# VectorE instead of GpSimd multiplies silu(gate) by the up projection in the last stage of a decoder layer

## The reference

```python
def _reorder_quantize_x(x, idx):
    scale = jnp.max(jnp.abs(x)) / GLOBAL_DIV
    xr = (x / scale)[:, idx]
    scale_x = jnp.max(jnp.abs(xr), axis=1, keepdims=True) / FP8_MAX
    qx = _fp8(xr / scale_x)
    return (qx, scale_x, scale)
...
qx, sx, sc = _reorder_quantize_x(xf, up_reorder_index)
g = _qlinear(qx, sx, sc, w_gate, up_reorder_index, out_idx=down_reorder_index)
u = _qlinear(qx, sx, sc, w_up, up_reorder_index, out_idx=down_reorder_index)
t = jax.nn.silu(g) * u
qt, st, sct = _reorder_quantize_x(t, down_reorder_index)
y = _qlinear(qt, st, sct, w_down, down_reorder_index)
...
x = x + _L0_attn_ref(_layernorm(x, axis=-1), ...)
x = x + _L0_xattn_ref(_layernorm(x, axis=-1), ctx_2048, mask_BxS2_bk0)
x = x + _L0_ffn_ref(_layernorm(x, axis=-1), ...)
```

## Time and profile before

| What | Value |
|---|---|
| Time before, median of 3 runs | 3047.39 us (3046.95 to 3049.8) |
| Profiled execution: time | 3048.07 us |
| Profiled execution: span | 3046.3 us |
| PE busy | 2735.2 us (90%) |
| DVE busy | 2197.3 us (72%) |
| ACT busy | 1124.8 us (37%) |
| POOL busy | 861.0 us (28%) |
| Mean granted TensorE clock | 0.944 |

### The profile page before, as it was taken

How to read it: one execution, slowest core, us unless ns; L and a number is a source line. 1 busy time by engine, 2 the same in 40 slices (tenths; PEclk the granted TensorE clock), 3 DMA queues, 4 the chain that set the end, 5 groups by cost and what they waited for, 6 DMA issues and landing times. The chain is left out here.

```text
span 3046.3 us, 40207 instructions
## 1 busy us (share of the span) xinstructions
PE 2735.2 (90%) x14796; PEld 2244.7 (74%) x14796; DVE 2197.3 (72%) x3911; ACT 1124.8 (37%) x1838; POOL 861.0 (28%) x815
## 2 busy tenths in 40 slices
PE   3289999999999999999999999996259999999985
PEld 1178888888888888888888888885146666666652
DVE  6567777677677777777777777775946888788785
ACT  2123333333333333333333333332544555555553
POOL 1211121121121121121112112113813666665665
PEclk7599999999999999999999999997579999999997
DMA  4533242333233233324233323322443343333410
GB/s 150 188 152 125 83 160 83 125 122 121 102 141 111 98 126 117 125 90 152 84 128 118 122 101 115 110 98 67 121 146 111 115 118 115 125 114 118 117 54 18
DMA packets 110754, 348.99 MB, mean 115 GB/s; under 512 B 12000, under 2 KB 12128, under 8 KB 101600
## 3 DMA queue, kind: packets, MB, share of 16 engines
q1 hardware_dynamic: 108224, 337.76, 32.0%
q0 software_dynamic: 2336, 8.65, 1.0%
HBM read 249.92 MB, written 96.47 MB: 114 GB/s over the span
## 5 line engine op out<-in xcount | busy, mean ns | idle before, releaser
L720 PE MATMUL bank<-attention_xT,attention_w_hi 128*128 128x512 f32 x3072 | 951.3, 391 | 9.5 <-POOL attention_w_lo L587 5.7
L620 POOL TENSOR_TENSOR attention_sq_sum<-attention_sq_sum,attention_sq 128x512 f32<-128x512 f32 x128 | 208.7, 1631 | 1609.8 <-ACT attention_sq L691 1609.8
L720 PEld LDWEIGHTS bank<-attention_xT,attention_w_hi 128*128 128x128 f32 x3072 | 569.3, 188 | 122.9 <-issue 11.1
L720 PE MATMUL bank<-attention_xT,attention_w_lo 128*128 128x512 f32 x1536 | 599.9, 391 | 0.0
L729 PE MATMUL bank<-attention_w_hi,attention_xT 128*128 128x256 f32 x2048 | 372.9, 283 | 2.6 <-DVE attention_vl L813 2.6
L1201 PE MATMUL bank<-w_out_hi,finish_og 128*128 128x512 f32 x1024 | 353.9, 408 | 8.3 <-DMA finish_og<-gated_heads 6.5
L720 PEld LDWEIGHTS bank<-attention_xT,attention_w_lo 128*128 128x128 f32 x1536 | 289.0, 188 | 62.5
L729 PEld LDWEIGHTS bank<-attention_w_hi,attention_xT 128*128 128x128 f32 x2048 | 317.7, 191 | 2.9 <-DVE attention_vl L813 2.8
L839 DVE TENSOR_TENSOR attention_sf<-bank,attention_dcy 128x512 f32<-128x512 f32 (+1 forms) x256 | 147.9, 619 | 218.4 <-PE bank L746 218.4
L729 PE MATMUL bank<-attention_w_lo,attention_xT 128*128 128x256 f32 x1024 | 289.4, 283 | 0.0
L858 DVE SCALAR_TENSOR_TENSOR attention_og<-bank,attention_nw,attention_gate 128x512 f32<-128x512 f32 x128 | 96.2, 751 | 255.7 <-PE bank L767 255.7
(11 more groups left out here) (194 smaller groups left out, 5134.2 us busy)
## 6 DMA issues: line engine op xcount, KB each, us to landing
attention_xT<-normed_turned SPq DMA_DIRECT2D x62, 2048.0 KB, 8.8
gated_heads<-attention_og_out SPq DMA_DIRECT2D x64, 1024.0 KB, 7.5
finish_og<-gated_heads SPq DMA_DIRECT2D x128, 512.0 KB, 3.8
normed_turned<-attention_xT SPq DMA_DIRECT2D x8, 2048.0 KB, 7.3
attention_og_out<-in_x SPq DMA_DIRECT2D x8, 1024.0 KB, 9.6
attention_raw<-in_w_head SPq DMA_DIRECT2D x16, 512.0 KB, 9.4
finish_x<-in_x SPq DMA_DIRECT2D x32, 256.0 KB, 4.3
out<-finish_x SPq DMA_DIRECT2D x32, 256.0 KB, 4.3
```

The costliest lines, as they stand in the source:

```text
L620: g.tensor_tensor(sq_sum[:, col], sq_sum[:, col], sq[:, :], ALU.add).then_inc(s_acc, 1)
L720: mm = pe.matmul(dst[:, :], part[a][w][:, k, col:col + P], xT[i][:, b, k, :], start=(k == 0 and s == 0), stop=(k == KD - 1 and s == 2))
```

## The change

The three products `silu_up(n, 0)`, `silu_up(n, 1)` and `silu_up(n, 2)` leave POOL's order. The same three instructions, with the same operands and the same waits, are issued by DVE: the first behind `x_scale(n + 2)` and ahead of the third `scaled_gate_up`, the second between `t_round_sum(n - 1)` and `t_round_out(n - 1)`, the third behind `denominator(n + 3)` and ahead of `t_scale(n)`. POOL keeps `silu`, `rstd` and `add_ffn`. Nothing else is edited.

```diff
                     if tile(n):
-                        silu_up(n, 0)
                         silu(n, 1)
-                        silu_up(n, 1)
                         silu(n, 2)
-                        silu_up(n, 2)
...
+                def silu_up(m, i):
+                    k, (a, w) = m * NF + i, FS[i]
+                    v.wait_ge(s_gs, k + 1)
+                    v.wait_ge(s_u, k + 1)
+                    if m:
+                        v.wait_ge(s_ts, m)
+                    v.tensor_tensor(t_[:, a:a + w], g_[k % 2][:, 0:w], u_[k % 2][:, 0:w], ALU.mult).then_inc(s_t, 1)
...
                         x_scale(n + 2)
                     if tile(n):
+                        silu_up(n, 0)
                         scaled_gate_up(n, 2)
                     if tile(n - 1):
                         t_round_sum(n - 1)
+                    if tile(n):
+                        silu_up(n, 1)
+                    if tile(n - 1):
                         t_round_out(n - 1)
...
                         denominator(n + 3)
                     if tile(n):
+                        silu_up(n, 2)
                         t_scale(n)
```

More of the change, by code:

```diff
@@ L1041, in silu @@
                     g.tensor_tensor(g_[k % 2][:, 0:w], g_[k % 2][:, 0:w], sg[k % 2][:, 0:w], ALU.mult).then_inc(s_gs, 1)
[L1043 to L1049, removed]
                 def rstd(n):
```

## The result

The changed kernel is slower: 3056.89 us, the median of 10 runs (3055.78 to 3059.41), against 3048.43 us for the kernel before in 10 runs. The ratio is 1.0027, with a 95% interval of 1.0018 to 1.0037. That is 8.5 us where 7.5 were forecast. The profiled execution took 3059.41 us with a span of 3057.7 us; it is the slowest of the ten, so the differences between the two traces add up to 11.4 us, not to 8.5.

What follows compares the result with a forecast made beforehand. A loop round all engines, not PE's 96.30 of 100 us busy, sets the 22.96 us step. 3.5 us over 27 steady steps plus 4.0 in the tail make 7.5, on the 3047.39 median 3055 us; range 3046 to 3083.

Steps and rivals of the forecast that it cites:

- The loop: Last stage's steady steps: a path round all engines, reciprocal to exponential, sets 22.96 us; the third product adds 0.59.
- The lock: DVE instructions with two SBUF operands exclude POOL; once waiting, POOL costs 1.13 or 0.86 us, DVE 0.55 or 1.48.
- The race: DVE's rounding sum at 13.19 against rstd's last POOL instruction at 13.21 for the lock, 0.02 us apart.
- the won race: Rounding sum goes before rstd's last instruction: steps 0.13 us longer, 23.09, 3.5 us over 27 steps; chance 0.45.
- the lost race: rstd's last instruction goes before the rounding sum: 1.06 us more a step, 3080, or 3065 for half; chance 0.37.
- The last steps and the end: Tail steps, without rstd and projection: 4.0 us more in all, from two steps at 1.4 and two at 0.6.
- the two steps put at 0.6 us each: The two tail steps before the two laid out: 0.6 us longer each, between nothing and 1.4.
- the two later ones, put at 1.4 each: Two tail steps: 11.66 us instead of 10.24 from y scaled to rounding output's end, 2.8 us together.
- PE's own limit: Steady step without PE's wait of 0.61 us for the rounded t: 22.35 us instead of 22.96.
- The faster rival: A plain DVE product needs no lock, so steady steps fall to 22.35 us: 16 us less, 3031; chance 0.13.

Runs made afterwards that it cites:

- third_ahead: The changed kernel with the third product moved ahead of the denominator, into DVE's wait for the exponential: 3040.43 us.
- third_only: The kernel before with only the third product on DVE, ahead of the row maximum, and the products' semaphore split in three: 3067.4 us.
- sum_later: The changed kernel with a DVE maximum over 64 columns, changing no result, ahead of the rounding sum: 3083.22 us.
- both_moved: The changed kernel with the second product behind the rounding output and the third ahead of the denominator: 3028.44 us.
- first_only: The kernel before with only the first product on DVE, ahead of the third scaled_gate_up, and the products' semaphore split in three: 3028.52 us.
- second_behind: The changed kernel with the second product behind the rounding output instead of ahead of it: 3042.45 us.
- pool_early: The kernel before, all products still on POOL, with the first product ahead of rstd in POOL's order: 3091.61 us.

## Why the prediction was right

The loop. It named the way from the reciprocal through `t_scale`, ACT, POOL's chain and the rounding output back to the exponential, not PE's 96% busy share, as what sets a step. `third_ahead` and `third_only` show it: 0.59 us taken off the loop or put on it move a step by 0.57 and 0.62 (0.51 against the base with the split semaphore).

The lock. Its prices (1.13, 0.86, 0.55 and 1.48 us once waiting) gave the step of the changed kernel as 23.09; it is 23.10. Each sign named for the won race is there: the new wait of 1.3 us, the `rstd` instruction of 1.6 us, `normed` 2.5 us later, the second product at 0.69.

The race. The margin of 0.02 us was forecast and found, and it held in all 27 steps, whose lengths lie between 23.08 and 23.11. The case of the lost race, 24.02 us a step and 3080 us in all, was made by `sum_later`: 24.13 and 3083. That the change itself came out on the forecast side is in part luck: the margin is no larger than what a few starts rounded to 0.01 us leave open, and the prediction gave the won race 0.45 and the lost one 0.37. The mechanism would have been as right with 3083.

The products. What the sum had as one figure is made of three of different sign. Taken singly against their base, the first brings 23 us, the second costs 36, and the third costs 16. Added up they would cost 29; together they cost 8.5. They are not additive: the second is dear alone (1.1 us a step) because POOL's third multiplication and third product both get in ahead of the output.

What was mis-sized. The last steps and the end cost 5.4 us in the traces, not 4.0. The step laid out instruction by instruction was exact (11.64 against 11.66). But by the starts of y scaled the two steps put at 0.6 us each cost 1.9 and 0.4, the two later ones, put at 1.4 each, 1.2 and 0.9, and the end 1.0, which the sum had at nothing. About 0.9 us of the 5.4 goes by PE's clock and not by the order of the products: the five down multiplications of the tail, 11 matmuls each, take 23.2 us together and took 22.3. The last one took 3.89 us at a granted clock of 0.65 and takes 4.87 at 0.50, the lower level; the one in the first of the four steps 3.78 at 0.67 and 4.90 at 0.50. The 0.6 us of the first step with a third product were left out of the sum.

PE's own limit is 22.15 us, not the 22.35 that the prediction had by taking PE's wait of 0.61 us off 22.96. The rows of the scores and of the turn of t, in the kernel before and in `both_moved`, show why:

```profile
2710.81 1.00 PE L1226 MATMUL bank<-finish_memT,finish_hT 128*128 128x64 f32 x8
```

```profile
2699.84 1.00 PE L1223 MATMUL bank<-finish_memT,finish_hT 128*128 128x64 f32 x8
2700.68 0.78 PE L1272 MATMUL bank<-ident_bf,down_named 128*128 128x128 bf16 x11
```

Without a wait the turn starts 0.84 us behind the start of the scores, inside their row. Before, it started 1.61 behind the earlier trace rows, so the wait cost 0.77 us and not 0.61. The faster rival's price of 16 us was too small by that; `both_moved` shows 20.

One reading was off without harm: `centred` lasts 0.78 us where nothing holds it, not 0.69. Its price of 0.55 once waiting was read from ends and stands.

The rival "faster" failed as it was put, since a plain product does need the lock. But the sign that it named was right: with the output ended before 18.4 us after the reciprocal (17.0 in `both_moved`, 17.1 in `first_only`) the step falls to PE's limit. In `second_behind`, at 17.6, it stops at 22.7, where PE waits for h. The products had only to stand elsewhere.

## What to carry to other kernels

Before moving an elementwise instruction with two SBUF operands between GpSimd and VectorE, lay out one step of the timeline with both engines in one column, and ask of each two-operand instruction who starts first and who is held. Put the moved instruction where its engine waits for something else, and keep it away from a chain of tiny instructions on the other engine, each of which can be held for the whole of a long one. A place that wins by 0.02 us is not a place to leave it: 0.13 us of harmless work cost 26 us here.

## What the runs showed of the hardware that was not expected

In the races shown here the earlier recorded start got the lock, down to 0.02 to 0.03 us: DVE's sum at 2710.41 beat POOL at 2710.43 in the changed kernel, POOL at 2706.70 beat DVE at 2706.73 in `second_behind`. And such a margin was stable, step after step, over a whole execution. The ten executions of the changed kernel, on the edge of a race, lie within 3.6 us; the edit of `sum_later` moved it by 26.

Zeroing one number per partition on DVE, 0.06 us by its row, put the next instruction back by less than 0.02 us (the rounding sum starts 0.53 us behind the scaling of u with it and without it), while a maximum over 64 columns (0.21 us) put it back by 0.13.

A wait of PE cost more than its row says, 0.77 us for a row of 0.61, since without it the next matmuls start before the row of the ones ahead has ended. And the granted clock fell behind a wait of 1.9 us in four steps of `pool_early` and not in the others, 1.7 us each time.
